# Mamba front of a seven-stage transformer kernel: ScalarE makes the first tap of the convolution, and the parts of softplus are taken in another order

## The chip, the cores and the metric
One core of one Trainium2 chip runs the whole program in one launch. The metric is the device time of that launch in microseconds (us). Five engines run their own instruction streams: TensorE (PE, with its weight loads shown as PEld), VectorE (DVE), ScalarE (ACT), GpSimd (POOL) and SyncE (SP), which here only issues DMAs. They meet at semaphores.

## The reference, cut to what matters
Four layers of attention and feed-forward on 2 x 1024 tokens of width 128. The first stage is a Mamba block on the layer-normalised input:

```python
xz = xn @ W_in;  u, z = split(xz)                       # 256 + 256 channels
conv = depthwise_conv1d(u, conv_w, kernel 4, left pad 3)
u2 = silu(conv + conv_b)
dt_lo, Bm, Cm = split(u2 @ W_xp)                        # 8, 16, 16
dt = softplus(dt_lo @ W_dt + b_dt);  A = -exp(A_log)
h_t = exp(dt_t * A) * h_{t-1} + (dt_t * u2_t) * B_t;  y_t = h_t . C_t
out = x + res * ((y + u2 * D) * silu(z)) @ W_out
```

## The kernel before
The Mamba stage (class `Mamba`, lines 450 to 1084) holds channels on the 128 partitions and time along the free dimension. Its front works in four items n = 0 to 3: n // 2 is the batch b, n % 2 the half of the 256 channels; a tile is 128 x 1024 fp32. The scan behind it works in 64 items i (two batches, two halves, 16 states).

The order of work on each engine is written out by hand in `pe` (L717 on), `dve` (L852 on), `act` (L996 on), `pool` (L1058 on) and `sp` (L568 on). Each engine runs its list strictly in that order; PSUM is used as four pairs of banks.

For each item the front does this:
- PE projects u (`project_u`, L617) into a bank pair: items 0 to 3 use pairs 1, 2, 3, 0. `project_z` (L625) makes z, `project_x` (L634) makes B, C and dt_lo for a batch, `project_dt` (L644) makes the argument of softplus. `project_x` of batch 0 waits for the second `silu_u`, that of batch 1 for the fourth.
- DVE makes the convolution of u in four passes from PSUM into SBUF (`conv_dve`): one multiplication by the tap of lag 0 (L793) and three multiply-adds by the lags 1 (L796), 2 (L796) and 3 (L798). Every pass waits for the one before it.
- ACT applies silu (`silu_u`, L917), and to z (`silu_z`, L937), and copies B, C and dt_lo out of PSUM (`rows_act`, L942).
- Softplus is computed as max(v,0) + log(1 + q) with q = exp(-|v|), and one correction of the logarithm. With l = Ln(1 + q) computed, it adds a Newton term with the inverse exp(-l): ACT makes |v| (`abs_act`, L947) and q (`exps_act`, L954); DVE makes max(v,0) (`relu_dve`, L803; ACT does so for items 2 and 3, `relu_act`, L932), then 1 + q and the rounding of it (`up_dve`, L808 and L810); ACT takes the logarithms of two items (`logs_act`, L961) and then the inverses of two (`inverses_act`, L969); DVE ends with four passes per item (`sum_dve`): add the logarithm (L817), multiply the rounding by the inverse (L820), subtract it (L822), multiply dt by u2 (L825). The last one raises the semaphore `du`.
- `copy_z` (L922) is ACT's copy of z of the second batch out of PSUM.

What is ahead of the scan: the broadcast loads of the B rows (`load_b`, L561, SP queue) wait for `du` of item 1. POOL makes the products dB = du * B (L1072) and a quarter of the products h * C (L1084). The product of scan item 0 needs `du` of item 0, those of items 1 and 2 need `du` of all four. DVE runs the scans (L889), ACT the decays exp(dt * A) into PSUM (L980), PE turns h (L671) and sums y (L701, L705). The scan's first item stands behind `sum_dve(3)` on DVE's list. `c_rows_pe` (L657) makes the C columns once all of u2 and all of the softplus arguments are read.

ACT's function tables change where Sqrt, Silu, Exp, Ln, Exp, Ln and Exp follow each other in its list (each an ACT_TABLE_LOAD); Copy, Identity, Abs and Relu need no change of table here.

Of the kernel before, what the change touches and what calls it, by code (L numbers as in the profile page):

```python
# [13 lines left out]
ACT = mybir.ActivationFunctionType  # L14
# [435 lines left out]
class Mamba:  # L450
# [7 lines left out]
    def __init__(self, k):  # L458
        self.k = k
        A = Arena(k.arena, 0, k.arena_cols)  # L460
        self.scr = scr = A.take(16384)
        parts = lambda at, n, m=1024: [scr[:, at + m * i:at + m * (i + 1)] for i in range(n)]
        self.Bs, self.Cs, self.dB, self.hh, self.hc = parts(0, 4), parts(4096, 2), parts(6144, 3), parts(9216, 3), parts(12288, 4)
        t0, t1 = parts(0, 6), parts(12288, 4) + [A.take(1024) for _ in range(2)]
        self.Bs += [A.take(1024) for _ in range(2)]
        self.ex, self.u_, self.l_ = ([t[2 * j:2 * j + 2] for t in (t0, t1)] for j in range(3))
        self.xn = scr[:, 12288:14336].rearrange("p (i d) -> p i d", d=128)
        early = Arena(k.W, 0, 12288)
        self.xnT = early.take(2048)
        self.w_in = early.take(512)  # L470
        of = lambda: [a.take(2048).rearrange("p (e t) -> p e t", e=2) for a in (early, A)]
        self.u2, self.sz, self.dt, self.du = of(), of(), of(), of()
        self.bc = A.take(2048).rearrange("p (b t) -> p b t", b=2)
        self.cT = A.take(256).rearrange("p (b n k) -> p b n k", b=2, n=16)
        self.wxp = A.take(2 * 104).rearrange("p (e c) -> p e c", e=2)
        self.wout = A.take(256).rearrange("p (e d) -> p e d", e=2)
        self.Am = A.take(32).rearrange("p (e n) -> p e n", e=2)
        self.Dd = A.take(256).rearrange("p (e c) -> p e c", e=2)
        self.sd, self.rs = A.take(32).rearrange("p (q i) -> p q i", q=2), A.take(32).rearrange("p (q i) -> p q i", q=2)
        self.p1, self.nm, self.eps = A.take(NT), A.take(NT), A.take(2)  # L480
        self.spare = A.at
        self.rows = k.nc.dram_tensor("bcrows", (2, 32, 1024), F32).ap()
        self.S = S = k.signals(
            g_win=16, g_wxp=16, g_wout=16, stats=6, eps=1, sd=4, rs=4, xnv=12, xnp=4, tp=4, fxv=2, fxa=2, Aexp=1, Aneg=1, Dd=2,
            ip=4, conv=4, u2=4, zp=4, sz=4, zcp=2, xp=2, bc=2, bw=32, cTm=1, cT=1,
            dtm=4, sabs=4, tm=2, tma=2, ex1=4, up1=4, ln=4, tq=4, tr=4, dt=4, du=4, p1=1, res=16,
            B0=176, B1=176, B2=192, B3=192, B4=160, B5=160, C0=128, C1=128, hT=96, dA=64, dB=64, scan=64, hcv=16, hca=64, hcp=16, acc=64,
            yd=4, gate=4, op=2, ox=2)
        k.g_x += [S.B2, S.B3]
        self.S = S = S._replace(B2=Sig(S.B2.name, S.B2.sem, S.B2.base + 16), B3=Sig(S.B3.name, S.B3.sem, S.B3.base + 16))  # L490
        self.ready = (S.stats, 6)
        self.ends = [(S.op, 2), (S.stats, 6), (S.res, 16), (S.dB, 64), (S.hcp, 16)]
# [294 lines left out]
    def conv_dve(self, e, w, n, pair):  # L787

        k, S, b, eb = self.k, self.S, n // 2, n % 2
        cw = k.s("conv_w").rearrange("p (e j) -> p e j", e=2)  # L790
        u, dst = k.pair(2 * pair).rearrange("p c t -> p (c t)"), self.u2[b][:, eb, :]
        w.wait_ge(S.ip, n + 1)
        w.mark(e.tensor_scalar(dst, u, cw[:, eb, 3:4], None, MUL))  # L793
        for j in (2, 1):
            w.own()
            w.mark(e.scalar_tensor_tensor(dst[:, 3 - j:1024], u[:, 0:1021 + j], cw[:, eb, j:j + 1], dst[:, 3 - j:1024], MUL, ADD))  # L796
        w.own()
        e.scalar_tensor_tensor(dst[:, 3:1024], u[:, 0:1021], cw[:, eb, 0:1], dst[:, 3:1024], MUL, ADD).then_inc(S.conv.sem, 1)  # L798
# [10 lines left out]
        w.wait_ge(S.up1, n + 1)  # L809
        e.scalar_tensor_tensor(self.ex[b][eb], self.u_[b][eb], 1.0, self.ex[b][eb], SUB, SUB).then_inc(S.tq.sem, 1)  # L810

    def sum_dve(self, e, w, n):
        S, b, eb = self.S, n // 2, n % 2
        dt = self.dt[b][:, eb, :]
        self.wait_m(w, n)
        w.wait_ge(S.ln, n + 1)
        w.mark(e.tensor_tensor(dt, dt, self.l_[b][eb], ADD))  # L817
        w.wait_ge(S.tr, n + 1)
        w.wait_ge(S.tq, n + 1)
        w.mark(e.tensor_tensor(self.ex[b][eb], self.ex[b][eb], self.u_[b][eb], MUL))  # L820
        w.own()
        e.tensor_tensor(dt, dt, self.ex[b][eb], SUB).then_inc(S.dt.sem, 1)  # L822
        w.wait_ge(S.dt, n + 1)
        w.wait_ge(S.u2, n + 1)
        e.tensor_tensor(self.du[b][:, eb, :], dt, self.u2[b][:, eb, :], MUL).then_inc(S.du.sem, 1)  # L825
# [28 lines left out]
    def dve(self, e, w):  # L854
        k, S = self.k, self.S
        self.stats_dve(e, w, 0)
        self.stats_dve(e, w, 1)
        self.norm_dve(e, w, 0)
        self.norm_dve(e, w, 1)
        self.stats_dve(e, w, 2)  # L860
        self.feature_dve(e, w, 0)
        self.stats_dve(e, w, 3)
        self.feature_dve(e, w, 1)
        self.norm_dve(e, w, 2)
        self.norm_dve(e, w, 3)
        w.wait_ge(S.rs, 4)
        e.tensor_scalar(self.p1, self.rs[:, 0, :], 1.0, None, ADD)
        e.scalar_tensor_tensor(self.nm, k.lnmv[:, :, 0], -1.0, self.rs[:, 0, :], MUL, MUL).then_inc(S.p1.sem, 1)
        for n, pair in enumerate((1, 2, 3, 0)):
            self.conv_dve(e, w, n, pair)  # L870
        for eb in range(2):
            e.tensor_scalar(self.Dd[:, eb, :], k.c("ident"), k.s("D_param")[:, eb:eb + 1], None, MUL).then_inc(S.Dd.sem, 1)
        self.relu_dve(e, w, 0, 1)
        self.relu_dve(e, w, 1, 2)
        self.up_dve(e, w, 0)
        self.up_dve(e, w, 1)
        self.sum_dve(e, w, 0)
        self.sum_dve(e, w, 1)
        self.up_dve(e, w, 2)
        self.up_dve(e, w, 3)  # L880
        self.sum_dve(e, w, 2)
        self.sum_dve(e, w, 3)
        for i in range(64):
            b, eb, n = self.item(i)
            w.wait_ge(S.dA, i + 1)
            w.wait_ge(S.dB, i + 1)
            if i >= 3:
                self.wait_read(w, i - 3)
            e.tensor_tensor_scan(self.hh[i % 3], k.pair(2 * (i % 2)).rearrange("p c t -> p (c t)"), self.dB[i % 3], 0.0, MUL, ADD).then_inc(S.scan.sem, 1)  # L889
            if n == 2 and i > 2:  # L890
                self.gate_dve(e, w, i // 16 - 1)
            if i and self.on_dve(i - 1):
                self.times_dve(e, w, i - 1)
            if i == 35:
                self.out_dve(e, w, 0)
            if i == 42:
                self.after.early_norm_dve(e, w)
        self.after.route_dve(e, w, 0)
        self.gate_dve(e, w, 3)
        self.after.disp.dve(e, w, 0)  # L900
        self.out_dve(e, w, 1)
        self.after.norm_dve(e, w)
        self.after.route_dve(e, w, 1)
        self.after.disp.dve(e, w, 1)


    def feature_act(self, e, w, c):
        k, S = self.k, self.S
        w.wait_ge(S.tp, c + 1)
        w.wait_ge(k.g_small, 16)  # L910
        e.activation(self.xnT[:, c * 512:(c + 1) * 512], k.b(c % 2), ACT.Identity, scale=k.s("ln_g"), bias=k.s("ln_b")).then_inc(S.fxa.sem, 1)

    def silu_u(self, e, w, n):
        k, S, b, eb = self.k, self.S, n // 2, n % 2
# [38 lines left out]
            w.wait_ge(S.sabs, n + 1)  # L953
            e.activation(self.ex[b][eb], self.ex[b][eb], ACT.Exp, scale=-1.0).then_inc(S.ex1.sem, 1)  # L954

    def logs_act(self, e, w, b):
        S = self.S
        for eb in range(2):
            n = 2 * b + eb
            w.wait_ge(S.up1, n + 1)  # L960
            e.activation(self.l_[b][eb], self.u_[b][eb], ACT.Ln).then_inc(S.ln.sem, 1)  # L961

    def inverses_act(self, e, w, b):
        S = self.S
# [30 lines left out]
    def act(self, e, w):  # L995
# [3 lines left out]
        for c in range(4):  # L999
            h = slice(4 * c, 4 * c + 4)  # L1000
            w.wait_ge(S.stats, c + 1)
            e.activation(self.sd[:, 0, h], k.lnmv[:, h, 1], ACT.Sqrt, bias=self.eps[:, 0:1])
            e.activation(self.sd[:, 1, h], k.lnmv[:, h, 1], ACT.Sqrt, bias=self.eps[:, 1:2], scale=1.0 + 1e-5).then_inc(S.sd.sem, 1)
        self.feature_act(e, w, 2)
        self.feature_act(e, w, 3)
        self.silu_u(e, w, 0)
        self.silu_z(e, w, 0, 1)
        self.silu_u(e, w, 1)
        self.silu_u(e, w, 2)
        self.rows_act(e, w, 0, 2)  # L1010
        self.silu_z(e, w, 1, 3)
# [2 lines left out]
        self.abs_act(e, w, 1, 2)  # L1014
        self.exps_act(e, w, 0)
        e.activation(self.Am, k.s("A_log"), ACT.Exp).then_inc(S.Aexp.sem, 1)
        self.rows_act(e, w, 1, 0)
        self.logs_act(e, w, 0)
        self.copy_z(e, w, 0, 3)
        self.inverses_act(e, w, 0)  # L1020
        w.wait_ge(S.Aexp, 1)
        e.mul(self.Am, self.Am, -1.0).then_inc(S.Aneg.sem, 1)
        for n, pair in ((2, 1), (3, 2)):
# [1 line left out]
            self.relu_act(e, w, n, pair)  # L1025
        self.exps_act(e, w, 1)
        self.copy_z(e, w, 1, 0)
        self.logs_act(e, w, 1)
        self.inverses_act(e, w, 1)
        self.decay(e, w, 0)  # L1030
        self.decay(e, w, 1)
# [3564 lines left out]
```

## Time and profile before

| | us |
|---|---|
| median of 3 runs | 1598.65 (1595.17, 1598.65, 1599.42) |
| the profiled execution, its own time | 1595.64 |
| its span in the trace | 1593.8 |
| busy PE / PEld | 1259.4 / 895.2 |
| busy DVE / ACT / POOL | 1022.7 / 789.9 / 694.3 |

The span runs from the first to the last instruction of the trace; 1.84 us of the execution's own time lie around it. The Mamba stage fills about the first 280 us, its front the first 80. Busy shares are averages over seven stages, so what the front is worth is read from the front itself: the chain of waits and the engines' timelines below.

### The profile page before, as it was taken

The numbers are of one execution on the slowest core, as the hardware profiler recorded it, in microseconds if no ns is written. First come the engines' busy times: TensorE is split into PE (matmuls) and PEld (weight loads), VectorE is DVE, ScalarE is ACT, GpSimd is POOL, SyncE is SP. The second block draws the span as 40 slices with busy tenths as digits, with TensorE's granted clock in tenths as the row PEclk, the third lists the DMA queues.
The fourth block names the chain that finished last, engine by engine and source line by source line (L and its number), as shares of the span: only waits on it lengthen the run. The fifth ranks groups of instructions, "written<-read, shape, count | busy, mean of one in ns | idle before, by whom it ended". The sixth has DMA issues, their size and how long they took to land.

```text
span 1593.8 us, 27288 instructions
## 1 busy us (share of the span) xinstructions
PE 1259.4 (79%) x10086; PEld 895.2 (56%) x10086; DVE 1022.7 (64%) x1915; ACT 789.9 (50%) x1629; POOL 694.3 (44%) x688
## 2 busy tenths in 40 slices
PE   5888989322776568877868669998999999985996
PEld 2577768312554234444446534455776777874996
DVE  7798986760111888878743554547976885642775
ACT  3788685210433237767742235555665565321442
POOL 1099996474666340001014330024870881043453
PEclk9689999655888669999979889998999999997999
DMA  6388692112221431211001141112000003001113
GB/s 220 122 263 304 219 339 104 33 49 65 79 78 50 172 130 54 68 43 47 17 16 34 56 158 55 35 37 75 1 1 1 1 1 159 1 29 46 46 45 99
DMA packets 75492, 133.48 MB, mean 84 GB/s; under 512 B 12755, under 2 KB 39830, under 8 KB 74720
## 3 DMA queue, kind: packets, MB, share of 16 engines
q1 hardware_dynamic: 66432, 115.45, 22.1%
q0 software_dynamic: 8064, 13.87, 2.7%
q10 hardware_dynamic: 864, 2.43, 0.4%
q8 instruction: 80, 1.31, 0.4%
q14 instruction: 52, 0.43, 0.1%
HBM read 95.70 MB, written 38.38 MB: 84 GB/s over the span
## 4 chain that ended last, share of the span: by engine, by line
PE 47%; issue 18%; DVE 13%; ACT 7%; POOL 6%; DMA 4%; SPq 4%; another core or an unknown queue 1%; POOLq 0%; DVEq 0%; ACTq 0%
PE ps L1907 6%; PE ps L4138 3%; POOL sb_arena L1072 3%; PE ps L2274 2%; DVE sb_arena L1973 2%; ACT sb_arena L2221 2%; PE ps L2257 2%; PE ps L2516 1%; PE ps L3219 1%; PE ps L4105 1%; PE ps L4106 1%; PE ps L4107 1%; PE ps L3190 1%; SPq L68 1%
## 5 line engine op out<-in xcount | busy, mean ns | idle before, releaser
L1973 DVE TENSOR_REDUCE sb_arena<-ps 128x2 f32<-128x1024 f32 (+2 forms) x192 | 211.4, 1131 | 56.9 <-PE ps L2502 31.9
L2221 ACT ACTIVATE sb_arena<-ps 128x512 f32<-128x512 f32 (+1 forms) x320 | 160.3, 554 | 56.3 <-PE ps L2274 52.6
L889 DVE TENSOR_TENSOR_SCAN sb_arena<-ps,sb_arena 128x1024 f32<-128x1024 f32 x64 | 144.1, 2279 | 13.6 <-ACT ps L980 12.7
L2005 POOL CAST sb_arena<-sb_arena 128x8 bf16<-128x8 f32 (+2 forms) x32 | 6.5, 203 | 287.4 <-DVE sb_arena L1973 146.1
L1907 PE MATMUL ps<-sb_arena 128*32 128x256 f32 (+3 forms) x1856 | 115.1, 355 | 0.4 <-ACT sb_arena L2455 0.2
L1633 POOL DMA_INDIRECT y<-sb_arena x80 | 77.7, 972 | 55.7 <-ACT sb_arena L1582 32.9
L1173 POOL DMA_INDIRECT xe<-sb_arena x80 | 79.7, 996 | 49.9 <-issue 29.1
L1072 POOL TENSOR_TENSOR sb_arena<-sb_Wreg,sb_arena 128x1024 f32<-128x1024 f32 x32 | 74.8, 2365 | 59.9 <-DMA sb_arena<-bcrows 51.4
L705 PE MATMUL ps<-sb_const,sb_arena 128*128 128x128 f32 x768 | 92.3, 278 | 0.0
L705 PEld LDWEIGHTS ps<-sb_const,sb_arena 128*128 128x128 f32 x768 | 90.2, 195 | 2.0 <-issue 2.0
L2274 PE MATMUL ps<-sb_arena 51*128 51x256 bf16 (+2 forms) x768 | 60.7, 249 | 28.7 <-ACT sb_arena L2221 28.0
L1072 POOL TENSOR_TENSOR sb_arena<-sb_arena 128x1024 f32<-128x1024 f32 x32 | 74.6, 2361 | 12.5 <-DVE sb_arena L889 11.4
L2455 ACT ACTIVATE sb_arena<-ps 128x768 f32<-128x768 f32 x64 | 50.2, 785 | 59.7 <-PE ps L2524 59.7
L991 ACT ACTIVATE sb_arena<-ps,sb_arena 128x128 f32<-128x128 f32 x256 | 69.9, 403 | 19.6 <-PE ps L671 19.6
L2257 PE MATMUL ps<-sb_arena 55*128 55x128 bf16 (+4 forms) x576 | 63.1, 296 | 18.3 <-DVE sb_arena L1973 11.9
L3926 POOL TENSOR_TENSOR sb_arena<-sb_arena 128x512 f32<-128x512 f32 x32 | 41.0, 1282 | 81.0 <-ACT sb_arena L3737 61.4
L4292 DVE TENSOR_TENSOR sb_arena<-sb_arena,ps 128x512 f32<-128x512 f32 x60 | 41.0, 688 | 50.2 <-PE ps L4107 26.1
L4423 POOL DMA_INDIRECT y<-sb_arena x44 | 42.9, 976 | 64.6 <-ACT sb_arena L4350 57.8
L671 PE MATMUL ps<-sb_const,sb_arena 128*128 128x128 f32 x384 | 53.9, 284 | 21.6 <-DVE sb_arena L836 10.4
L1482 DVE TENSOR_TENSOR sb_arena<-sb_arena,ps 128x320 f32<-128x320 f32 x32 | 15.6, 488 | 85.6 <-remote 28.9
L1907 PEld LDWEIGHTS ps<-sb_arena 128*32 128x32 f32 x1856 | 45.6, 110 | 35.4 <-issue 12.1
L671 PEld LDWEIGHTS ps<-sb_const,sb_arena 128*128 128x128 f32 x384 | 44.6, 146 | 35.0 <-issue 25.4
(526 smaller groups left out, 3491.0 us busy)
## 6 DMA issues: line engine op xcount, KB each, us to landing
sb_arena<-bcrows SPq DMA_DIRECT2D x80, 512.0 KB, 6.6
xe<-sb_one SPq DMA_DIRECT2D x31, 260.0 KB, 6.7
sb_Wreg<-e0w SPq DMA_DIRECT2D x24, 256.0 KB, 7.6
sb_arena<-xe SPq DMA_DIRECT2D x16, 325.0 KB
y<-sb_zero SPq DMA_DIRECT2D x20, 256.0 KB, 6.6
sb_arena<-y SPq DMA_DIRECT2D x4, 1024.0 KB, 8.9
sb_Wreg<-e1w SPq DMA_DIRECT2D x16, 256.0 KB, 2.8
sb_Wreg<-e3gu SPq DMA_DIRECT2D x1, 4096.0 KB, 14.2
```

The lines of the kernel that those rows point to most:

```text
L671: t = e.transpose(k.b(self.C + c)[:, j * 128:(j + 1) * 128], self.hh[i % 3][:, at:at + 128], k.c("ident"))
L705: t = e.matmul(k.b(self.Y + c)[:, at:at + 128], self.hc[i % 4][:, x * 128:(x + 1) * 128], k.c("ident"), start=False, stop=False)
L889: e.tensor_tensor_scan(self.hh[i % 3], k.pair(2 * (i % 2)).rearrange("p c t -> p (c t)"), self.dB[i % 3], 0.0, MUL, ADD).then_inc(S.scan.s ...
L991: t = e.activation(self.hc[i % 4][:, x * 128:(x + 1) * 128], k.b(self.C + c)[:, j * 128:(j + 1) * 128], ACT.Identity, scale=self.cT[:, b, ...
L1072: e.tensor_tensor(self.dB[i % 3], self.du[b][:, eb, :], self.Bs[i % 6], MUL).then_inc(S.dB.sem, 1)
L1173: e.indirect_dma_start(buf, bass.IndirectOffsetOnAxis(self.iw[:, c:c + 1], 0), xn[q][:, i, :], None, bounds_check=rows - 1, oob_is_err=Fal ...
L1633: e.indirect_dma_start(self.y, bass.IndirectOffsetOnAxis(at, 0), self.ob[u % 3][:, c, :], None, bounds_check=8191, oob_is_err=False).then_ ...
L1907: t = e.matmul(k.b(self.sum_bank(qc))[32 * j:32 * j + 32, o:o + wd], self.vaug[:, b * 8 + kt, 4 * hg + j, :], self.PT[x][:, j, a - q0:a - ...
L1973: e.tensor_reduce(dst, src, AX.X, MAX).then_inc(S.mxr.sem, 1)
L2221: e.activation(self.PT[s % 4][:, 2 * h:2 * h + 2, 0:n], bank[:, :, 0:n], ACT.Exp, scale=self.scale).then_inc(S.ex.sem, 1)
L2257: t = e.matmul(view[:, p, a:z], Q[r, j % 2, tok], KK[r, j % 2, k0 + a:k0 + z], start=True, stop=True, skip_group_check=True)
L2274: t = e.matmul(banks[h][:, j, a:z], KK[r, j, kt * 128:(kt + 1) * 128], Q[r, j, q0 + a:q0 + z], start=True, stop=True, skip_group_check=True)
```

## The change
ScalarE makes the tap of lag 0 (`tap_act`, an Identity activation with the tap as scale, from the u pair into the same SBUF tile) and DVE starts each convolution with its second pass, waiting for a new semaphore `tap` in place of `ip`. The multiply-add of lag 1 no longer waits for a pass of DVE's own. `logs_act` (both items of a batch) becomes `log_act` (one item); the copy of the rows of batch 1 stands between the two logarithms of batch 0, and the copy of z of item 2 behind the inverses in place of ahead of them. `silu_u` of item 1 comes ahead of `silu_z` of item 0. The addition of the logarithm leaves `sum_dve` and becomes `add_log_dve`; both additions of a batch stand ahead of both sums.

```diff
     def conv_dve(self, e, w, n, pair):
-        w.wait_ge(S.ip, n + 1)
-        w.mark(e.tensor_scalar(dst, u, cw[:, eb, 3:4], None, MUL))
+        w.wait_ge(S.tap, n + 1)
         for j in (2, 1):
-            w.own()
+            if j == 1:
+                w.own()
             w.mark(e.scalar_tensor_tensor(dst[:, 3 - j:1024], u[:, 0:1021 + j], cw[:, eb, j:j + 1], dst[:, 3 - j:1024], MUL, ADD))
...
+    def add_log_dve(self, e, w, n):
+        S, b, eb = self.S, n // 2, n % 2
+        dt = self.dt[b][:, eb, :]
+        self.wait_m(w, n)
+        w.wait_ge(S.ln, n + 1)
+        w.mark(e.tensor_tensor(dt, dt, self.l_[b][eb], ADD))
+
     def sum_dve(self, e, w, n):
-        self.wait_m(w, n)
-        w.wait_ge(S.ln, n + 1)
-        w.mark(e.tensor_tensor(dt, dt, self.l_[b][eb], ADD))
         w.wait_ge(S.tr, n + 1)
         w.wait_ge(S.tq, n + 1)
...
         self.up_dve(e, w, 0)
         self.up_dve(e, w, 1)
+        self.add_log_dve(e, w, 0)
+        self.add_log_dve(e, w, 1)
         self.sum_dve(e, w, 0)
         self.sum_dve(e, w, 1)
         self.up_dve(e, w, 2)
         self.up_dve(e, w, 3)
+        self.add_log_dve(e, w, 2)
+        self.add_log_dve(e, w, 3)
         self.sum_dve(e, w, 2)
         self.sum_dve(e, w, 3)
...
+    def tap_act(self, e, w, n, pair):
+        k, S, b, eb = self.k, self.S, n // 2, n % 2
+        cw = k.s("conv_w").rearrange("p (e j) -> p e j", e=2)
+        w.wait_ge(S.ip, n + 1)
+        w.wait_ge(k.g_small, 16)
+        e.activation(self.two(self.u2[b][:, eb, :]), k.pair(2 * pair), ACT.Identity, scale=cw[:, eb, 3:4]).then_inc(S.tap.sem, 1)
...
+        self.tap_act(e, w, 0, 1)
         self.feature_act(e, w, 2)
         self.feature_act(e, w, 3)
+        self.tap_act(e, w, 1, 2)
         self.silu_u(e, w, 0)
+        self.tap_act(e, w, 2, 3)
+        self.silu_u(e, w, 1)
         self.silu_z(e, w, 0, 1)
-        self.silu_u(e, w, 1)
+        self.tap_act(e, w, 3, 0)
         self.silu_u(e, w, 2)
         self.rows_act(e, w, 0, 2)
         self.silu_z(e, w, 1, 3)
...
         e.activation(self.Am, k.s("A_log"), ACT.Exp).then_inc(S.Aexp.sem, 1)
+        self.log_act(e, w, 0)
         self.rows_act(e, w, 1, 0)
-        self.logs_act(e, w, 0)
+        self.log_act(e, w, 1)
+        self.inverses_act(e, w, 0)
         self.copy_z(e, w, 0, 3)
-        self.inverses_act(e, w, 0)
...
         self.copy_z(e, w, 1, 0)
-        self.logs_act(e, w, 1)
+        self.log_act(e, w, 2)
+        self.log_act(e, w, 3)
         self.inverses_act(e, w, 1)
```

## Rows read from the trace of the kernel before

**Rows 1.** Chain of waits, 14 to 82 us: start, length, engine and line.
```profile
28.84 1.16 ACT sb_Wreg L917
...
30.13 5.02 PE ps L634 x8
...
41.14 6.33 PE ps L634 x8
...
51.72 0.99 ACT sb_arena L922
...
79.22 2.35 POOL sb_arena L1072
```

**Rows 2.** Stretches: length, busy PE, PEld, DVE, ACT, POOL, PEclk, DMA share, GB/s.
```profile
26.00:29.00 3.00, 0.61 (x2) 0.00 (x0) 2.93 (x4) 1.18 (x2) 0.00 (x0) 1.00 0.02 7
30.00:33.00 3.00, 2.87 (x4) 1.23 (x5) 2.90 (x3) 0.00 (x0) 0.00 (x0) 0.52 0.00 0
82.00:90.00 8.00, 5.75 (x26) 4.75 (x25) 7.89 (x5) 6.11 (x15) 8.00 (x4) 0.50 0.80 253
80.00:180.00 100.00, 88.45 (x636) 75.64 (x636) 90.00 (x47) 84.07 (x191) 100.00 (x44) 0.95 0.79 263
```

**Rows 3.** DVE's timeline, convolution of items 0 and 1.
```profile
18.43 1.28 DVE L793 TENSOR_SCALAR sb_Wreg<-ps,sb_small 128x1024 f32<-128x1024 f32 x1 [1.66 <-PE ps L617]
19.75 2.60 DVE L796 SCALAR_TENSOR_TENSOR sb_Wreg<-ps,sb_small,sb_Wreg 128x1023 f32<-128x1023 f32 x2
...
23.58 1.27 DVE L793 TENSOR_SCALAR sb_Wreg<-ps,sb_small 128x1024 f32<-128x1024 f32 x1
```

**Rows 4.** PE's timeline: the projections of u for items 1 to 3.
```profile
19.58 5.32 PE L617 MATMUL ps<-sb_Wreg 128*128 128x512 f32 x12
```

**Rows 5.** ACT's timeline, 20 to 58 us.
```profile
20.75 1.28 ACT L917 ACT_TABLE_LOAD   x1
...
40.18 2.11 ACT L947 ACTIVATE sb_arena<-ps,sb_small 128x1024 f32<-128x1024 f32 x2
...
47.49 1.01 ACT L942 COPY sb_arena<-ps 104x1024 f32<-104x1024 f32 x1 [1.77 <-PE ps L634]
...
54.03 2.00 ACT L969 ACTIVATE sb_arena<-sb_arena 128x1024 f32<-128x1024 f32 x2
```

**Rows 6.** DVE's timeline, the sums and what stands around them.
```profile
58.78 1.22 DVE L817 TENSOR_TENSOR sb_Wreg<-sb_Wreg,sb_arena 128x1024 f32<-128x1024 f32 x1
59.91 1.22 DVE L820 TENSOR_TENSOR sb_arena<-sb_arena 128x1024 f32<-128x1024 f32 x1
...
63.57 0.69 DVE L808 TENSOR_SCALAR sb_arena<-sb_arena 128x1024 f32<-128x1024 f32 x1
...
67.30 1.22 DVE L817 TENSOR_TENSOR sb_arena<-sb_arena 128x1024 f32<-128x1024 f32 x1
69.61 2.22 DVE L820 TENSOR_TENSOR sb_arena<-sb_arena 128x1024 f32<-128x1024 f32 x1 [1.09 <-ACT sb_arena L969]
...
79.05 2.28 DVE L889 TENSOR_TENSOR_SCAN sb_arena<-ps,sb_arena 128x1024 f32<-128x1024 f32 x1
```

**Rows 7.** ACT's timeline, second batch: a logarithm, then the inverses.
```profile
66.15 1.06 ACT L961 ACTIVATE sb_arena<-sb_arena 128x1024 f32<-128x1024 f32 x1 [0.81 <-DVE sb_arena L808]
...
68.52 2.00 ACT L969 ACTIVATE sb_arena<-sb_arena 128x1024 f32<-128x1024 f32 x2
```

**Rows 8.** POOL's and the SP queue's timeline: B's load and the first product.
```profile
63.74 1.76 SPq L561 DMA_DIRECT2D sb_arena<-bcrows  x4
...
68.08 2.67 POOL L1072 TENSOR_TENSOR sb_arena<-sb_Wreg,sb_arena 128x1024 f32<-128x1024 f32 x1 [51.45 <-DMA sb_arena<-bcrows]
```

**Rows 9.** PE's timeline: eight turns of h at each clock.
```profile
81.48 1.94 PE L671 MATMUL ps<-sb_const,sb_arena 128*128 128x128 f32 x8 [7.37 <-DVE sb_arena L889]
...
93.74 1.04 PE L671 MATMUL ps<-sb_const,sb_arena 128*128 128x128 f32 x8
94.61 1.95 PE L705 MATMUL ps<-sb_const,sb_arena 128*128 128x128 f32 x16
```

More of the change, by code:

```diff
@@ L484, in __init__ @@
             g_win=16, g_wxp=16, g_wout=16, stats=6, eps=1, sd=4, rs=4, xnv=12, xnp=4, tp=4, fxv=2, fxa=2, Aexp=1, Aneg=1, Dd=2,
-            ip=4, conv=4, u2=4, zp=4, sz=4, zcp=2, xp=2, bc=2, bw=32, cTm=1, cT=1,
+            ip=4, tap=4, conv=4, u2=4, zp=4, sz=4, zcp=2, xp=2, bc=2, bw=32, cTm=1, cT=1,
             dtm=4, sabs=4, tm=2, tma=2, ex1=4, up1=4, ln=4, tq=4, tr=4, dt=4, du=4, p1=1, res=16,
@@ L810, in up_dve @@
         e.scalar_tensor_tensor(self.ex[b][eb], self.u_[b][eb], 1.0, self.ex[b][eb], SUB, SUB).then_inc(S.tq.sem, 1)
-    def sum_dve(self, e, w, n):
+    def add_log_dve(self, e, w, n):
         S, b, eb = self.S, n // 2, n % 2
@@ L817, in sum_dve @@
         w.mark(e.tensor_tensor(dt, dt, self.l_[b][eb], ADD))
+    def sum_dve(self, e, w, n):
+        S, b, eb = self.S, n // 2, n % 2
+        dt = self.dt[b][:, eb, :]
         w.wait_ge(S.tr, n + 1)
@@ L954, in exps_act, with log_act @@
             e.activation(self.ex[b][eb], self.ex[b][eb], ACT.Exp, scale=-1.0).then_inc(S.ex1.sem, 1)
[L956 to L961, printed above, removed]
+    def log_act(self, e, w, n):
+        S, b, eb = self.S, n // 2, n % 2
+        w.wait_ge(S.up1, n + 1)
+        e.activation(self.l_[b][eb], self.u_[b][eb], ACT.Ln).then_inc(S.ln.sem, 1)
     def inverses_act(self, e, w, b):
```

## The prediction, made before the kernel was run
> **What bounds the kernel now.** I read the chain of waits over the front first. It runs through every engine in turn: PE's projection of u, the convolution on DVE, the second silu on ACT, then without a gap PE's projection of x for batch 0, that of z, that of dt and that of x for batch 1 (30.13, then to 41.14 + 6.33 = 47.47), ACT's copies, logarithms and inverses, DVE's sums, and POOL's second product dB at 79.22 [rows 1]. So the front is a serial chain, and a microsecond taken out of it starts the scan a microsecond sooner. Then I ask whether the scan passes that on. The row by stretch for 80 to 180 us shows POOL busy 100.00 of 100 us with 44 products, DVE at 90, ACT at 84 and PE at 88 [rows 2]. From its second product on, the stage runs at POOL's pace, so it ends as much earlier as that product starts earlier. Nothing behind it waits for a fixed time: the loads and clearings of the SP queue wait for products, gates or earlier stages. I take the shift at full value to the end.
>
> **The taps.** DVE's four passes of a convolution take 18.43 to 23.58, a pitch of 5.15; the last three take 19.75 to 23.58, a pitch of 3.83 [rows 3]. Four tap passes leave DVE and four activations of 1024 columns from PSUM come to ACT. The trace has no Identity of that shape; the nearest is |v| with a bias, two in 2.11, so 1.06 each [rows 5]. The bounds are 1.0 (the copy of rows) and 1.28 (the pass on DVE); I take 1.06. What stands behind the taps on ACT's list:
> - Tap 0 starts at 18.43 as DVE's pass did [rows 3] and ends at 19.5, so convolution 0 gains about 0.2. The two feature copies behind it end near 21.0. PE's twelve matmuls for items 1 to 3 start at 19.58 and take 0.43 each [rows 4]; those of item 2, which read the copies, come at 21.3.
> - Tap 1 needs the second u (19.58 + 4 x 0.43 + a drain of 0.17 = 21.5 [rows 4]) and ends at 22.6. The table load, which stands at 20.75 now [rows 5], moves to 22.6 and ends at 23.85. Silu 0 starts there, 0.35 behind the end of convolution 0. This is covered: the projection of x waits for silu 1.
> - Convolution 1 runs 23.4 to 27.3. Tap 2 ends at 26.0, tap 3 (behind silu 1 and silu z) near 30.6; DVE wants them at 27.3 and 31.1. The least margin is 0.5.
>
> Silu 1 starts at 27.4 in place of 28.84 [rows 1]: 1.45 earlier, two convolutions at 1.32 each less handed back at the first tap. The projection of x then starts at 28.7. Convolutions 2 and 3 end at 31.2 and 35.0, ahead of PE, which has the projection of x until 33.7. So the whole chain down to q of item 1 moves by **-1.45**. A further 2.6 us off DVE (items 2 and 3) gives nothing, since PE is in the chain there.
>
> By the Trainium skill's page "ScalarE: Activation LUTs", section "Rules for kernel authors", a multiplication belongs on VectorE and not on ScalarE, which speaks against this move. Here the DVE pass is 1.28 and ACT's nearest 1.06 [rows 3, 5]: ACT is no slower on fp32 from PSUM, and it idles between the silus. The sum would lose the 1.45 only if the tap were in the chain each time.
>
> **Logarithm ahead of the rows' copy.** Today ACT idles 1.77 until the projection of x for batch 1 is done (47.49), copies, loads a table, takes two logarithms, copies z (0.99), loads, and starts the inverses at 54.03 [rows 1, 5]. In the new order the load and one logarithm come first: 45.72 - 1.45 = 44.27, plus 1.28 and 1.06, is 46.6, and the projection is done at 47.47 - 1.45 = 46.0. The idle 1.77 is gone, with 0.6 in hand, and the copy of z (0.99) stands behind the inverses: **-2.76**. The number of table loads is unchanged. PE's projections of dt for batch 1 wait for the rows' copy, 46.6 to 47.6 in place of 47.49 to 48.5, so they come earlier too.
>
> **Additions out of the sums.** Both additions of batch 0 fit between the logarithms and the first inverse (46.95 to 49.8; the inverse ends at 50.9). The first sum already had its addition in the shade, the second saves one pitch, 59.91 - 58.78 = **1.13** [rows 6]. The last pass of item 1, now ended at 63.57 [rows 6], ends at 63.57 - 1.45 - 2.76 - 1.13 = 58.2.
>
> **The second batch.** The copy of z now runs ahead of its |v| passes, so ACT's lead is 4.21 - 0.99 = 3.22. The logarithm of item 3 waited 0.81 for DVE [rows 7]; DVE is earlier by 5.3, so this wait goes too. The inverses start at 68.52 - 3.22 - 0.81 = 64.5 and the first correction at 69.61 - 4.03 = 65.6. From that pass (69.61) to the scan (79.05) are 9.44 us [rows 6]. Of these 1.13 is item 3's addition, now ahead, and 1.00 a stall: the pass took 2.22 where its twin took 1.22 [rows 6]. Without both the scan would start at 65.6 + 7.31 = 72.9.
>
> **The stall does not go; it moves.** The loads of B wait for item 1's du, 63.57, and the first product starts 4.51 later at 68.08 [rows 8]. It takes 2.67 against 2.35 for a plain one [rows 1, 8], and it starts while an addition (67.30 to 68.52) runs. So either engine holds the other up for about a whole instruction. Next time du is at 58.2 and the product wants to start at 62.75, between the two additions (62.2 to 64.5). If POOL goes second it runs 63.4 to 65.75, the second addition to 66.9 and the correction starts then. If DVE keeps both additions, POOL runs 64.5 to 66.85 and the correction is held until then. Both put it 1.3 after 65.6. The bounds are 0 (the product lands clear of DVE) and 2.35 (one whole product). Scan at 72.9 + 1.3 = 74.2, against 79.05.
>
> The Trainium skill's page "SBUF — State Buffer", section "SBUF: two separate sides", says that VectorE with two SBUF inputs and GpSimd take a shared pair of ports as an exclusive lock for a whole instruction, first come first. The trace agrees, by the 1.00 above. If they only divided bandwidth, the 1.3 would spread over the passes and could be less.
>
> **Sum.** Along the chain that ends last: -1.45 (taps), -2.76 (order of logarithms and copies), +0.99 (copy of z now ahead of batch 1), -0.81 (ACT's wait for DVE) make -4.03 at the first correction of batch 1; then -1.13 (addition of item 3), -1.00 (the stall of now) and +1.30 (the stall to come): **-4.86** at the scan, 74.2 in place of 79.05. Against the profiled execution's own time, 1595.64, this makes 1590.8. That execution is 3.0 under the median of the runs, 1598.65; on the median it is **1593.8**, 0.30% less. Some 0.3% (4.8 us) is also about what a measurement of this kernel can tell from no change, so the likeliest case stands just on that line.
>
> **Rivals.**
> - *The clock of PE holds.* PE is now idle from 26.6 to 30.13 and the granted clock falls to 1.2 GHz; for 30 to 33 it is 0.52 [rows 2], and the projection of x takes 5.02 [rows 1]. After the change the idle time is 2.1. If the clock stays at 2.4 GHz, eight matmuls at 0.43 and a drain give 3.6, 1.4 less: -6.26, 1592.4. For it: the clock was still 1.00 in 26 to 29 [rows 2]. [...] Chance 0.16.
> - *The product misses DVE's passes*, through a load that lands sooner or later: -6.16, 1592.5. Against it, four loads are issued at once and DVE has little idle time. Chance 0.12.
> - *Part is given back*: the clock falls later and covers all of the projection, 6.33 as in batch 1 [rows 1] in place of 5.02, or a tap or copy comes late by as much: -3.55, 1595.1 (-4.86 + 1.31). Chance 0.25.
> - *Slower.* At the start of the scan PE runs at 1.2 GHz (0.50 in 82 to 90 [rows 2]); eight turns take 1.94 against 1.04, and the sixteen matmuls of a sum, 1.95 at full clock [rows 9], would take twice that. An item so costs PE 2.85 more, while POOL still had no idle time. If the earlier start kept the clock low for longer, PE would fall behind POOL. Clearly slower means losing 4.86 + 4.8 = 9.66, 3.4 more items at that pace, some 19 us more at half clock. Chance 0.04, and 1603.5 or more.
> - That the edit does not do what it says has little room: the waits are explicit. It is inside the case of part given back.
>
> **Chances and range.** The likeliest case has 0.43, and a little over half of it lies beyond 0.3%. Faster by over 0.3%: 0.16 + 0.12 + 0.25 = 0.53. Within: 0.18 + 0.25 = 0.43. Slower by over 0.3%: 0.04. For the range, all gains together are -4.86 - 1.4 - 1.3 = -7.56 (1591.1) and the least is 1595.1; the runs of before spread over 4.25, half of which goes on either side: 1589.0 to 1597.3.
>
> **What would show it.** Right: DVE's multiply-adds (L796) start at about 19.6 and the convolutions follow at 3.83; silu 1 at 27.4; the projection of x at 28.7; no idle time ahead of the copy of rows of batch 1; inverses at 49.8 and 64.5; B's loads at 58.4; a DVE pass of over 2 us near 65; the scan at 74 and POOL busy from then on as now. The prediction is wrong if taps make DVE wait beyond the first, if the projection of x takes other than 5 us, if the additions come behind the inverses, or if the end of the Mamba stage moves by other than the start of its scan.

## The result and the profile after

| | before | changed |
|---|---|---|
| median of 17 runs each | 1592.47 us | 1585.44 us |
| lowest to highest | 1587.77 to 1601.38 | 1578.18 to 1592.89 |
| profiled execution, its span | 1595.64, 1593.8 | 1592.66, 1590.8 |

The ratio is 0.9963 (95% interval 0.9946 to 0.9981), some 5.9 us less: faster by 0.37%, with 0.2 to 0.5% inside the interval. The forecast difference, 0.30%, is a ratio of 0.9970 and inside the interval. The forecast time, 1593.8, and its range, 1589.0 to 1597.3, were missed: the 17 runs of before have their median 6.2 under that of the three runs known at the time, and the changed kernel came out at 1585.44.

The chain of waits of the changed kernel over the front (start, length, engine and line):

```profile
18.53 1.12 ACT sb_Wreg L927
...
19.68 1.29 DVE sb_Wreg L796
...
27.45 1.16 ACT sb_Wreg L933
...
28.74 5.35 PE ps L634 x8
34.09 1.72 PE ps L625 x4
35.81 3.64 PE ps L644 x8
...
39.47 1.12 ACT sb_arena L963
...
49.56 2.00 ACT sb_arena L983 x2
...
61.88 0.90 DVE sb_arena L817
...
73.78 2.17 POOL sb_arena L1092
```

The second silu, 28.84 before [rows 1], starts at 27.45, the projection of x at 28.74 in place of 30.13, GpSimd's second product at 73.78 in place of 79.22. PE's projection of x for batch 1 has left the chain: the softplus of batch 0 reaches ACT by another way, through the |v| pass (L963), since the first logarithm no longer stands behind the rows' copy. The copy itself (L958, 46.30) is still in it, between the two logarithms, but nothing waits ahead of it.

DVE's timeline of the same kernel, for [rows 6]:

```profile
57.97 0.69 DVE L808 TENSOR_SCALAR sb_arena<-sb_arena 128x1024 f32<-128x1024 f32 x1
...
61.88 4.51 DVE L817 TENSOR_TENSOR sb_arena<-sb_arena 128x1024 f32<-128x1024 f32 x2
66.32 1.21 DVE L824 TENSOR_TENSOR sb_arena<-sb_arena 128x1024 f32<-128x1024 f32 x1
...
73.62 2.28 DVE L897 TENSOR_TENSOR_SCAN sb_arena<-ps,sb_arena 128x1024 f32<-128x1024 f32 x1
```

The inverses of batch 0 start at 49.56 (in the chain above), 54.03 before [rows 5]. The sum of item 1 is over at 57.97 (63.57 before [rows 6]), and the pass that took 2.22 before [rows 6] takes 1.21; the stall is now in the two additions of batch 1, 4.51 where the same two take 2.36 undisturbed (the kernel with the product kept clear, below). GpSimd's first product is what they meet:

```profile
62.48 2.84 POOL L1092 TENSOR_TENSOR sb_arena<-sb_Wreg,sb_arena 128x1024 f32<-128x1024 f32 x1 [45.74 <-DMA sb_arena<-bcrows]
```

**Where the time went behind the front.** The whole span shrank by 3.0 in these two profiles, while the first scan moved by 5.43. Times at which passes of DVE and ACT that end a stage are done, in the two profiles and in three further ones from the experiments below (us):

| | before | changed | changed, 2nd | changed, 3rd | changed, 4th |
|---|---|---|---|---|---|
| first scan starts | 79.05 | 73.62 | 73.69 | 73.45 | 73.61 |
| last scan done | 275.26 | 269.18 | 269.23 | 268.89 | 269.26 |
| first mixture of experts done | 540.04 | 529.66 | 534.78 | 537.31 | 529.41 |
| causal attention done (ACT) | 809.22 | 804.71 | 802.24 | 810.78 | 795.73 |
| last stage's additions start | 1585.20 | 1582.23 | 1581.57 | 1591.60 | 1574.67 |

The front and the scan repeat to 0.4 us. What follows does not, with not a line altered: the third and the fourth profile of the changed kernel agree to 0.4 at 269 us and differ by 17 at the end. Of the 10.4 us by which the changed kernel led when the mixture of experts was done, 4.3 were gained behind the scan, and 5.9 were lost again by the end of the attention; both are of this kind: in the four profiles of the changed kernel the mixture of experts took 260.1 to 268.4 behind the last scan and the attention 266.3 to 275.0, and the 264.8 and 269.2 of before lie inside.

### The profile page after: what moved, and what is told of

The parts are those of the page before. It is cut to its first block, busy times and chain, and to the rows that moved or that the text cites. A ratio compares the mean times of both kernels' runs of the same rounds, so it can differ in the third digit from the quotient of the medians.

```text
span 1590.8 us, 27288 instructions
## 1 busy us (share of the span) xinstructions
PE 1262.5 (79%) x10086; PEld 894.4 (56%) x10086; DVE 1019.2 (64%) x1911; ACT 794.1 (50%) x1633; POOL 695.0 (44%) x688
## 4 chain that ended last, share of the span: by engine, by line
PE 46%; issue 22%; DVE 12%; ACT 7%; POOL 6%; DMA 4%; SPq 2%; another core or an unknown queue 1%; POOLq 0%; DVEq 0%; ACTq 0%
PE ps L1927 6%; POOL sb_arena L1092 4%; PE ps L4158 3%; PE ps L2294 3%; DVE sb_arena L1993 2%; ACT sb_arena L2241 2%; PE ps L2277 2%; PE ps L3239 1%; PE ps L2536 1%; PE ps L4125 1%; PE ps L4126 1%; PE ps L4127 1%; PE ps L3210 1%; PE ps L3169 1%; PE ps L4144 1%
```

## The experiments

### The three parts, one at a time
Each is the kernel before with one part of the change; the three together are the changed kernel.

**Taps alone** (ScalarE makes the lag 0 tap, with the new order of silus):

```diff
-        w.wait_ge(S.ip, n + 1)
-        w.mark(e.tensor_scalar(dst, u, cw[:, eb, 3:4], None, MUL))
+        w.wait_ge(S.tap, n + 1)
...
+        self.tap_act(e, w, 0, 1)
         self.feature_act(e, w, 2)
```

> Only the taps are moved to ScalarE. Serial-chain theory: the second silu starts 1.4 earlier than the 28.84 of before, the inverses of batch 0 at 52.0 to 52.6 (before 54.03), the first scan 1.4 to 2.1 earlier than 79.05. Rival (ScalarE is in the way): VectorE idles before its multiply-adds beyond the first convolution and the scan starts at 79 or later. The whole time should move by the same 1.4 to 2.1 if the shift is passed on.

Ratio 0.9985 (0.9958 to 1.0012). The first scan started at 74.46: 4.6 earlier, not 1.4 to 2.1. Its chain of waits:

```profile
27.27 1.16 ACT sb_Wreg L925
...
28.56 3.65 PE ps L634 x8
32.21 1.72 PE ps L625 x4
33.93 3.63 PE ps L644 x8
37.56 5.32 PE ps L634 x8
42.90 1.01 ACT sb_arena L950
```

The silu is about where it was expected (27.4). The rest is PE's: the projection of x takes 3.65 where it took 5.02 [rows 1], that of dt 3.63 for 4.27, that of x for batch 1 5.32 for 6.33. These are the same matmuls at another granted clock, 1.00 over 28 to 32 us (columns as in [rows 2]) where before had 0.69:

```profile
28.00:32.00 4.00, 3.44 (x8) 1.47 (x9) 3.93 (x4) 3.24 (x4) 0.00 (x0) 1.00 0.00 0
```

With the 1.6 of the silu, 1.6 + 1.4 + 0.6 + 1.0 is the 4.6; the last of these counts here because the logarithms still stand behind the projection for batch 1. So 1.6 of the 4.6 comes straight from the taps and 3.0 by the clock, and the shifts of the three parts can't be added. VectorE does not wait for a tap after the first.

**Order of logarithms and copies alone:**

```diff
-        self.rows_act(e, w, 1, 0)
-        self.logs_act(e, w, 0)
-        self.copy_z(e, w, 0, 3)
+        self.log_act(e, w, 0)
+        self.rows_act(e, w, 1, 0)
+        self.log_act(e, w, 1)
         self.inverses_act(e, w, 0)
+        self.copy_z(e, w, 0, 3)
```

> Only the order of logarithms, rows' copy and z copy. Serial-chain theory: no idle time ahead of the rows' copy of batch 1; inverses of batch 0 at 51.3 (2.76 earlier), du of item 1 at 60.8, inverses of batch 1 at 65.9, the stall of one VectorE pass stays near 1.0, the first scan at 76.5 (2.6 earlier). Rival (the logarithm is not ready early, or the projection is): less than 1.5 earlier.

Ratio 0.9983 (0.9957 to 1.0008). The scan started at 76.47, expected 76.5. From its chain of waits:

```profile
47.24 0.27 ACT sb_arena L959
...
48.20 0.56 ACT sb_arena L942
...
51.46 2.00 ACT sb_arena L967 x2
...
67.04 2.22 DVE sb_arena L820
```

The logarithm, the rows' copy, the logarithm and the inverses follow each other without a wait; the inverses start 2.57 earlier, in a profile whose first convolution began 0.2 later. The stall (2.22) is where it was.

**Additions alone:**

```diff
         self.up_dve(e, w, 1)
+        self.add_log_dve(e, w, 0)
+        self.add_log_dve(e, w, 1)
         self.sum_dve(e, w, 0)
```

> Only the additions are moved out of the sums. Serial-chain theory: inverses of batch 0 unchanged at 54.0, du of item 1 1.13 earlier at 62.4, inverses of batch 1 0.8 earlier at 67.7; the first product of GpSimd lands between the two additions of batch 1 and costs them about 2.1 more than their 2.3; first scan near 78.2, 0.85 earlier. If the ports are not exclusive, the additions take 2.3 and the scan starts near 76.1.

Ratio 0.9982 (0.9956 to 1.0008). DVE's timeline:

```profile
55.47 1.23 DVE L824 TENSOR_TENSOR sb_arena<-sb_arena 128x1024 f32<-128x1024 f32 x1 [1.78 <-ACT sb_arena L977]
...
62.78 0.69 DVE L808 TENSOR_SCALAR sb_arena<-sb_arena 128x1024 f32<-128x1024 f32 x1
...
66.51 4.53 DVE L817 TENSOR_TENSOR sb_arena<-sb_arena 128x1024 f32<-128x1024 f32 x2
...
78.26 2.28 DVE L897 TENSOR_TENSOR_SCAN sb_arena<-ps,sb_arena 128x1024 f32<-128x1024 f32 x1
```

The scan at 78.26, expected 78.2; the two additions at 4.53 show the stall moved into them by this part alone. That the times agree so closely is partly luck: in this profile the convolutions began 0.13 later and PE's projections took longer, and the rows' copy came 0.35 later than before (47.84), so the part itself gave 1.1, not the 0.85 of the expectation. The three whole times are each within noise of before: parts of 1 to 3 us can't be told apart there, and what is said of the parts rests on the start of the scan.

### The taps undone
The changed kernel with the taps back on VectorE, and with them the old order of the silus.

> The changed kernel with the taps back on VectorE; logarithms, copies and additions as changed. Serial-chain theory: what the taps are worth on top of the rest, 1.45 if the clock of TensorE is as in the two profiles: second silu at 28.9, first scan 75.0 to 75.6. If the projection of x happens to run at the full clock (3.65), up to 1.6 less.

Ratio 0.9986 (0.9962 to 1.001). Second silu at 28.63, scan at 75.54, so on top of the rest the taps are worth 1.8 to 2.1 against the four profiles of the changed kernel in the table. Of this, 1.2 is the silu and 0.7 PE's projection of x, which took 6.08 here, the longest of all, for 5.35; that of dt took 3.64. The first convolution began at 18.21 here, 0.3 ahead of the first tap of the changed kernel (18.53), so the taps' own worth is 1.5.

### GpSimd's first product kept clear
```diff
-            w.wait_ge(S.du, 4 if i in (1, 2) else 2 * b + eb + 1)
+            w.wait_ge(S.du, 4 if i in (0, 1, 2) else 2 * b + eb + 1)
```

> The changed kernel, in which GpSimd's first product waits for du of all four items, so that it can't meet VectorE's passes. If the two engines exclude each other over whole instructions: the two additions of batch 1 take 2.4 in place of 4.51, the first correction of batch 1 starts at 65.1 in place of 66.3, the last du is done at 72.5 (73.7); GpSimd's first product then runs 72.5 to 74.9 and the second starts at 74.9, 1.1 later than 73.78, and the scan ends 1.1 later. Rival (the slow addition has another cause, as the loads of the B rows): the additions still take over 4.

Ratio 0.9988 (0.9966 to 1.0011). The times of the front all lie some 1.7 under those expected, because PE's clock held in this profile (projection of x 3.65, as with the taps alone). DVE's and POOL's timelines:

```profile
61.29 1.22 DVE L817 TENSOR_TENSOR sb_arena<-sb_arena 128x1024 f32<-128x1024 f32 x1
63.39 1.23 DVE L824 TENSOR_TENSOR sb_arena<-sb_arena 128x1024 f32<-128x1024 f32 x1 [0.88 <-ACT sb_arena L983]
```
```profile
70.87 13.89 POOL L1092 TENSOR_TENSOR sb_arena<-sb_Wreg,sb_arena 128x1024 f32<-128x1024 f32 x6 [54.17 <-DVE sb_arena L829]
```

With no product about, the addition takes 1.22, DVE waits 0.88 for the inverse, and the correction starts as soon as that is there. In the changed kernel the inverses start at 64.04, so it could have started at 65.1 and started at 66.3: the stall costs 1.2. The loads of the B rows ran at the same time here too, issued 3.74 ahead of the first addition as in the changed kernel, so it is the product and not the loads. Keeping it clear costs more than it saves: the first product then starts at 70.87 and the second 2.3 later at 73.2, where the changed kernel with this clock would start it at 72.0 (its 73.78 less the 1.73 by which |v| of item 1 was earlier here, 37.74 for 39.47).

### TensorE kept busy
The projection of z of item 0 is made twice over, only to fill the gap ahead of the projection of x.

```diff
-        for c in range(2):
+        for c in (0, 1, 0, 1) if n == 0 else range(2):
```

> The changed kernel with the projection of z of item 0 made twice over, four matmuls in place of two, so that TensorE idles some 0.2 in place of 1.95 ahead of the projection of x of batch 0. Theory (TensorE's clock prices the projection, which is in the chain): granted clock 1.00 over 28 to 32, that projection takes 3.65 in place of 5.35, the exponentials start 1.7 earlier, the first scan at 71.9 in place of 73.6 and the end of the stage 1.7 earlier. Rival (the clock falls anyway, or another wait ends last): first scan 73.3 or later.

Ratio 0.9962 (0.9941 to 0.9982). Chain of waits, then the stretch of 28 to 32 us in the busy times (columns as in [rows 2]):

```profile
28.76 3.65 PE ps L634 x8
32.41 1.72 PE ps L625 x4
34.13 4.36 PE ps L644 x8
38.51 1.11 ACT sb_arena L963
```
```profile
28.00:32.00 4.00, 3.92 (x10) 1.46 (x9) 3.93 (x4) 3.35 (x4) 0.00 (x0) 1.00 0.00 0
```

The clock stayed at 1.00 and the projection took 3.65, 1.7 less, as the theory has it. But the clock fell later, within the projections of dt (4.36 for 3.64), and 0.7 was lost again: |v| at 38.51 in place of 39.47, scan at 72.66, expected 71.9.

### The kernel before once more

> The kernel before once more, nothing altered: how much of its profile repeats. First scan at 79.05 if TensorE's clock falls as it did, down to 76 if it holds over a projection; the stretch from the first to the last scan 196.2 within 0.5. Theory (levels of the whole time come from stages behind this one): the stretches behind the scan differ from the first profile by 2 us or more in at least two stages. Rival (they are fixed): all within 1 us.

Ratio 1.0009 (0.9985 to 1.0032), on a chip on which all kernels run at another level: 1567 us for this one, 1559 to 1565 for the three variants above. First scan 79.43, last scan done at 275.69: 196.3 from one to the other, as before. The first mixture of experts was done at 521.61, after 245.9 in place of 264.8 in the first profile. So all of the 30 us between the two profiles lie behind this stage, 18.9 of them in that one, 4.6 in the attention and the rest behind. The four profiles from this chip have 245.9 to 246.6 for the mixture of experts, the ten others 260.1 to 270.3.

### The changed kernel, three times more
The runs of before are on the same chip each time.

> The changed kernel once more, nothing altered: what of its profile repeats. Theory (the front is all of the change, the level of a run is not its doing): first scan again at 73.6 within 0.3; the end of the stage again 5.5 to 6.1 earlier than in the profile of before; the further 4 us that the first mixture of experts ran shorter in the changed kernel's profile, and the 5 us that the causal attention ran longer, do not both repeat within 1 us. Rival (the edit reaches into later stages): both repeat. The whole time stands 5 to 6 us under the kernel before on the same chip, whatever the level of both.

Ratio 0.9949 (0.9926 to 0.9973).

> The changed kernel a third time. The question is what TensorE's clock does over the projection of x of batch 0. Theory (with 2.0 of idle time ahead of it the clock holds in some executions and falls in others, while with 3.3 or more it always fell): that projection takes either 3.65 or over 5, and the second product starts at 72.0 or at 73.8 accordingly; nothing else in the front differs by over 0.2. Rival (the front has one time): 73.8 again.

Ratio 0.9985 (0.9962 to 1.0008).

> The changed kernel a fourth time, for the same question as the third: the projection of x of batch 0 takes 3.65 or over 5, and the second product of GpSimd starts at 72.0 or at 73.8 accordingly.

Ratio 0.997 (0.9945 to 0.9994). All three have the projection of x at 5.35 and the second product at 73.85, 73.61 and 73.77; the question to the last two was whether the clock ever holds in this very kernel, and it did not. (The idle times in the expectation of the third are round: 2.0 stands for 1.3 to 2.3, and "3.3 or more" was 3.08 or more.) These two are the last columns of the table above, with the largest difference at the end. The busy times of the third and fourth profile over 530 to 800 us, where the causal attention runs:

```profile
530.00:800.00 270.00, 213.45 (x2708) 104.34 (x2708) 225.23 (x312) 176.57 (x353) 46.93 (x113) 0.90 0.19 59
```
```profile
530.00:800.00 270.00, 210.52 (x2829) 105.22 (x2828) 219.53 (x297) 185.68 (x370) 46.13 (x112) 0.95 0.19 58
```

In the same code the granted clock was 0.90 in the one and 0.95 in the other, and the stage 273.5 and 266.3 us long (from the table). Taken over each profile's own stretch of the stage, the clock was 0.90, 0.91, 0.93, 0.94 and 0.95 where it took 275.0, 273.5, 269.2, 267.5 and 266.3 (the changed kernel, its third profile, before, the second and the fourth), with VectorE busy for 218.1 to 218.3 in all five. That these go together is seen; that the clock is the cause was not tried.

### The first B rows loaded early
GpSimd's first product follows du of item 0, from a tile that nothing used before.

```diff
-        self.Bs += [A.take(1024) for _ in range(2)]
+        self.Bs = [A.take(1024) for _ in range(2)] + self.Bs
...
-        w.wait_ge(S.du, 2)
+        w.wait_ge(S.du, 2 if i > 1 else 0)
```

> The changed kernel, in which the first two B rows get the two tiles that nothing else used before and are loaded without waiting for du; GpSimd's first product then follows du of item 0 and meets VectorE's sum of item 1, where VectorE has 1.1 to spare. Theory (the stall of the additions is exclusion by GpSimd's product, and costs the chain 1.2): first product at 54.3, a pass of the sum of item 1 takes up to 2.4 more or the product waits, the two additions of batch 1 take 2.4, the first correction of batch 1 starts within 0.2 of the end of the inverse, second product at 72.6 with the clock fallen (projection of x 5.35) or 71.0 with it held (3.65): 1.1 under the changed kernel in the same state. Rival (VectorE has nothing to spare there): no gain, second product at 73.7 or 72.0.

Ratio 0.9973 (0.9955 to 0.9991). The clock held (3.65 again). POOL's and ACT's timelines:

```profile
52.75 3.28 POOL L1092 TENSOR_TENSOR sb_arena<-sb_Wreg,sb_arena 128x1024 f32<-128x1024 f32 x1 [36.05 <-DVE sb_Wreg L829]
71.81 11.59 POOL L1092 TENSOR_TENSOR sb_arena<-sb_Wreg,sb_arena 128x1024 f32<-128x1024 f32 x5 [15.78 <-DVE sb_arena L829]
```
```profile
60.87 1.06 ACT L975 ACTIVATE sb_arena<-sb_arena 128x1024 f32<-128x1024 f32 x1 [0.80 <-DVE sb_arena L808]
```

The pass of VectorE that the first product met:

```profile
53.84 3.27 DVE L826 TENSOR_TENSOR sb_Wreg<-sb_Wreg,sb_arena 128x1024 f32<-128x1024 f32 x1
```

The additions took 2.35 as expected, but the second product came at 71.81, only 0.2 under the 72.0 of this clock. The product held a pass of the sum of item 1 (3.27 in place of 1.22), DVE was 2 us late with 1 + q, and ACT's logarithm of item 3 waited 0.80 for it, the same wait that the change had removed. VectorE had the 1.1 to spare that I gave it, but it was held for 2.05, and the other 0.9 reached ACT: the inverses of batch 1 start at 63.24, where they start at 62.30 with the product kept clear and the same clock. That eats most of the 1.2 that the additions win. My sum had left it out, and the outcome is near the rival's.

### Both

> Both the early rows and the doubled projection of z of item 0. Theory (the two gains are in different parts of the chain and add up): projection of x of batch 0 at 3.65, second product at 71.7, 1.1 under the 72.82 of the doubled projection alone; if the clock doesn't fall over the projections of dt (3.64 in place of 4.4), 71.0. Rival (one gain hides the other): 72.5 or later.

Ratio 0.9965 (0.9941 to 0.9988). Projection of x 3.65, of dt 3.69, second product at 71.64. It is what the early rows gave alone (71.81, in a profile that began 0.16 later), where the clock held over the projection without doubled matmuls. Against the 72.82 of the doubled projection alone it is 1.2 less, of which 0.7 is the clock over the projections of dt and 0.2 an earlier start. Here the clock held also over PE's projection of x for batch 1, 3.68, for 5.3 to 6.6 in all other profiles; that stands outside the chain. So they do not add up as I had it. No version was shown to beat the changed kernel in the whole time: 0.9962, 0.9965 and 0.9973 have intervals that all contain its own.

## Why the prediction was right and wrong

**The step that failed is the last: "on the median it is 1593.8", and the range about it.** The sum was made in differences, and then set on the median of three runs, with half of their spread of 4.25 to either side (by that sum the upper end is 1597.2, not 1597.3). The same kernel's 17 runs span 13.6 and their median is 1592.47; on the three chips of the later comparisons it is 1567.97, 1597.19 and 1598.21. The forecast difference, set on 1592.47, would have been 1587.6; 1585.44 is 2.2 under that, and the least of the range was 1589.0. The same range about 1587.6, from 1582.8 to 1591.1, would have held it. Of the 2.2, 0.6 is the front and 0.65 the scan in the profiles (below); the remaining 1.0 is inside the interval of the ratio, 2.9 us to either side. A range for a time had to hold the level of the chip and of the run, which three runs do not show. As a ratio the forecast holds: 0.9970 against 0.9963 (0.9946 to 0.9981), and over three further comparisons 0.9949, 0.9985 and 0.997.

Step by step, forecast against the changed kernel's profile:

| step | forecast | measured |
|---|---|---|
| second silu | 27.4 | 27.45 |
| projection of x starts | 28.7 | 28.74 |
| \|v\| of item 1 and the exponentials | -1.45 | -1.70 |
| inverses of batch 0 (order) | 49.8 | 49.56 |
| B's loads | 58.4 | 58.14 |
| a DVE pass over 2 us, stall | near 65, 1.3 | the two additions, 4.51, 1.2 |
| inverses of batch 1 | 64.5 | 64.04 |
| first scan | 74.2 (-4.86) | 73.62 (-5.43) |
| last scan done | as the scan's start | -6.08 |

- **Taps, mis-sized by 0.25.** The start of the projection moved by 1.39. The projections of x, z and dt then took 10.7 in place of 11.0 (5.02 + 1.72 + 4.27 [rows 1]), with PE's clock low over other matmuls than before. I held PE's durations fixed while their times moved. The taps themselves cost ACT 1.10 to 1.12 each, forecast 1.06, for 1.28 on VectorE, and only the first is in the chain.
- **Order, right.** -2.77 for -2.76, shown alone by the order experiment (76.47 for 76.5).
- **Additions, right**, shown alone, including the stall's move into them (4.53); the agreement of the scan's start to 0.06 was luck in part. Two additions take 4.51 with the product about and 2.36 without. In all thirteen profiles in which a pass of VectorE met the first product, the pass ended 1.08 or 1.09 behind the product (here 62.48 + 2.84 = 65.32, and 61.88 + 4.51 = 66.39), whenever the product had begun: the pass did all its work behind it. Had the two divided a bandwidth, this distance would differ with their overlap. So the exclusive lock of the Trainium skill's page "SBUF — State Buffer", section "SBUF: two separate sides", named ahead, is what these traces show.
- **ACT's wait for DVE, mis-sized by 0.1.** The two logarithms of batch 1 took 2.92 from start to end before and take 2.00 now (60.72 on), so 0.92 is gone, not 0.81. The stall to come was 1.2, not 1.3. With 0.25 for the taps and 0.1 each for this wait, the stall and the copy of z, the sum of -4.86 becomes -5.4; -5.43 was measured.
- **Copy of z, mis-sized by 0.1.** It stands between other passes of ACT, which overlap it: the next one starts 0.90 behind it, not 0.99.
- **The shift passes through the scan, right within what repeats.** The last scan is done 6.08 earlier, 0.65 more than its first start moved. From GpSimd's second product to the end of the last scan it was 196.0 before and 195.4 after; over all twelve experiments it lies between 194.7 and 196.3, so 0.65 is no sign of the change.
- **The rival "the clock of PE holds" is real**; its chance of 0.16 can't be judged by so few profiles. The projection of x took 3.65 in three of the seven profiles with the taps on ScalarE and nothing added to TensorE's work (taps alone, product kept clear, early rows), 5.35 in the other four, and 5.02 to 6.08 in all five with the taps on VectorE. Against the changed kernel's profile it is worth 1.7 in the front; against the durations of my sum 2.0 (3.65 + 1.72 + 3.64 for 5.02 + 1.72 + 4.27), where I had 1.4, since I left out the matmuls behind. The gap ahead of the projection alone does not sort them. It was 1.95, 2.16, 2.26 and 2.26 where the clock fell, and 1.33, 1.37 and 2.29 where it held; in all five profiles with the taps on VectorE it was 3.08 to 4.00, and the clock fell. A projection of other than 5 us was, by the prediction's own words, a sign of its being wrong, and three variants show it. All four profiles of the very changed kernel show a fall, so that it gains more in some of its executions is likely but not shown.

The projection in the fourth profile of the changed kernel and in the one with the early rows:

```profile
28.71 5.35 PE L634 MATMUL ps<-sb_Wreg,sb_arena 128*104 128x512 f32 x8 [2.26 <-ACT sb_Wreg L933]
```
```profile
28.71 3.65 PE L634 MATMUL ps<-sb_Wreg,sb_arena 128*104 128x512 f32 x8 [1.37 <-ACT sb_Wreg L933]
```

- **The other rivals were not seen.** The product met the additions in all four profiles of the changed kernel (it began at 62.12 to 62.71). Of "part is given back" there was a quarter, the projection of x at 5.35 for 5.02, and the shorter projection of dt made up for it; no tap came late. For "slower", POOL had no idle time at the start of the scan.

## What to carry to other kernels
A serial front could be predicted from the rows to 0.6 us by following which instruction each one stands behind; the same forecast as a whole time is only as good as the level of the run, so give it as a ratio, and judge parts of 1 to 3 us by a mark inside the trace that repeats, here the start of the scan. When an instruction is moved, ask which pass of the neighbour engine it now meets: a stall by exclusion moved with the load that triggers it, and went on costing the chain 0.9 to 1.9 us wherever the product met a pass. And where TensorE idles ahead of a matmul in the chain, take the matmul's duration at both clocks.

## What the runs showed that I had not expected
- The same code, on the same chip, agrees to 0.4 us over its first 269 us and differs by 17 at the end (1585.10 and 1602.04). Between chips it is 30, 18.9 of it in the first mixture of experts.
- TensorE's clock fell or held over a projection behind 1.3 to 2.3 us of idle time, at 1.00 or at 0.64 to 0.72 over 28 to 32 us in the same instructions. With that gap filled, the fall moved to the next matmuls in one profile (4.36 in place of 3.64) and came only behind 45 us in the other.
- A product on GpSimd of 2.35 took 2.47 to 3.28 when it met VectorE's passes, and held those for 1.0 to 2.2, each pass ending 1.08 or 1.09 behind it; where it met none (kept clear) neither was longer than usual.
